# Node work of an attention pass cut into pieces behind the next round's groups, and matmuls of zeros left out

## What is computed

```python
h = (x @ W).reshape(N, H, D)                       # N = 12500, H = 4, D = 64
alpha = leaky_relu(a_src[src] + a_dst[dst], 0.2)   # per edge and head, self loops too
alpha = exp(alpha - amax[dst])
alpha = alpha / (segment_sum(alpha, dst)[dst] + 1e-16)
out = segment_sum(h[src] * alpha[:, :, None], dst)
x = layernorm(x + (out.reshape(N, H*D) + bias) @ Wl + bl)
```

## Time and profile before

| | us |
|---|---|
| median of 3 runs | 9799.77 (9795.94 to 9801.96) |
| the profiled execution | 9789.83, its span 9788.2 |
| attention pass, first to last aggregation (L844) | 204 to 2722 of the span |
| PE busy in the whole span | 6498.4 (66%) |
| POOL | 4718.8 (48%) |
| DVE | 4539.3 (46%) |
| ACT | 1864.8 (19%) |

### The profile page before, as it was taken

The page is one execution under the profiler, slowest core; times in us unless marked ns, Lnnn a source line. Parts: engine busy times, 40 slices in busy tenths (PEclk is TensorE's granted clock), DMA queues, the critical chain, the costliest instruction groups (busy, mean ns, idle before and its releaser), DMA issues.

```text
span 9788.2 us, 254659 instructions
## 1 busy us (share of the span) xinstructions
PE 6498.4 (66%) x65048; PEld 4741.4 (48%) x65049; DVE 4539.3 (46%) x11895; ACT 1864.8 (19%) x3800; POOL 4718.8 (48%) x4467
## 2 busy tenths in 40 slices
PE   4888777777726666665778866675776455455676
PEld 3666555555512221112444555664675454454566
DVE  4555555555578877774443333332222232232333
ACT  1433333333311334552000000000000000000000
POOL 2777666565500000004762036544764775774765
PEclk7888888888868889998889987887888677677788
DMA  2444444443310112334566566675776677677676
GB/s 56 100 97 95 94 91 94 92 89 87 87 33 39 79 80 116 131 138 171 174 185 191 177 221 203 221 230 172 226 253 209 208 276 266 207 259 243 211 268 231
DMA packets 973391, 1566.40 MB, mean 160 GB/s; under 512 B 499841, under 2 KB 621441, under 8 KB 966402
## 3 DMA queue, kind: packets, MB, share of 16 engines
q1 hardware_dynamic: 485762, 1244.14, 36.9%
q0 software_dynamic: 150016, 196.43, 9.7%
q10 hardware_dynamic: 337280, 122.87, 4.8%
HBM read 1337.91 MB, written 225.00 MB: 160 GB/s over the span
## 4 chain that ended last, share of the span: by engine, by line
PE 33%; issue 22%; DVE 15%; DVEq 11%; POOL 10%; DMA 7%; ACT 2%; ACTq 1%; SPq 0%; POOLq 0%
PE ps_turn L999 15%; POOL ARENA L671 10%; PE ps_turn L954 5%; PE ps_out L844 4%; DMA ARENA<-edge_attr 3%; DMA ARENA<-counts 2%; DVE ARENA L1886 2%; DVE ARENA L1884 2%; PE ps_pair L844 2%; PE ps_turn L817 1%; PE ps_pair L1021 1%; DVEq L1891 1%; DVEq L1981 1%; DVE ARENA L1981 1%; DVE DSUM L2050 1%
## 5 line engine op out<-in xcount | busy, mean ns | idle before, releaser
L999 PE MATMUL ps_turn<-ARENA 128*128 128x192 bf16 (+2 forms) x28812 | 2810.5, 267 | 834.6 <-DVE DSUM L2050 397.0
L999 PEld LDWEIGHTS ps_turn<-ARENA 128*128 128x128 bf16 x28812 | 2355.8, 108 | 1297.4 <-issue 996.4
L671 POOL DMA_INDIRECT ARENA<-table_sage,idx x1920 | 2013.1, 1048 | 1143.4 <-issue 963.6
L671 POOL DMA_INDIRECT ARENA<-table_gat,idx x1568 | 1693.8, 1080 | 851.9 <-issue 480.0
L954 PE MATMUL ps_turn<-ARENA 128*128 128x392 bf16 (+1 forms) x4204 | 1063.8, 359 | 679.7 <-DVE ARENA L1886 407.0
L671 POOL DMA_INDIRECT ARENA<-table_dev,idx x480 | 492.2, 1025 | 1616.6 <-ACT idx L1220 1472.3
L1884 DVE TENSOR_SCALAR ARENA<-ARENA 128x784 bf16<-128x784 f16 (+1 forms) x2102 | 1009.2, 480 | 363.5 <-issue 238.1
L954 PEld LDWEIGHTS ps_turn<-ARENA 128*128 128x128 bf16 (+1 forms) x4204 | 335.6, 101 | 1407.7 <-issue 1364.8
L671 POOL DMA_INDIRECT ARENA<-table_gine,idx x480 | 500.9, 1043 | 847.1 <-issue 684.0
L1202 ACT ACTIVATE ARENA<-ps_turn 128x784 f32 x784 | 645.9, 824 | 1086.4 <-PE ps_turn L954 1086.1
L2050 DVE TENSOR_REDUCE DSUM<-ps_turn 128x64 f32<-128x192 f32 (+2 forms) x686 | 263.9, 385 | 1171.7 <-PE ps_turn L999 966.3
(11 more groups left out here) (320 smaller groups left out, 5616.5 us busy)
## 6 DMA issues: line engine op xcount, KB each, us to landing
ARENA<-counts SPq DMA_DIRECT2D x1764, 448.0 KB
counts<-ARENA SPq DMA_DIRECT2D x49, 3136.0 KB, 9.0
ARENA<-counts SPq DMA_DIRECT2D x588, 224.0 KB
ARENA<-dst_b SPq DMA_DIRECT2D x393, 256.0 KB
ARENA<-edge_attr ACTq DMA_DIRECT2D x392, 128.0 KB
ARENA<-table_sage,idx POOLq DMA_INDIRECT x1920
ARENA<-table_gat,idx POOLq DMA_INDIRECT x1568
nodes_dev<-table_rows ACTq DMA_DIRECT2D x14, 672.0 KB
```

The lines of the kernel that those rows point to most:

```text
L671: pool.indirect_dma_start(ps["buf"][:, s, c, 0:ps["row"]], None, ps["table"][:, :], bass.IndirectOffsetOnAxis(idx[:, s, c:c + 1], 0)).then ...
L999: last = pe.matmul(ps_dense[half][:, 0:n], RING[:, b, :], XP[:, b, :], start=(b == PIECE_AT[pieces[0]]), stop=(j == pieces[-1] and b == PI ...
```

## The change

1. `fill` and its calls are gone: PE waits without matmuls of zeros in front of its waits.
2. The second half of a block's node work is owed (a register `owed` on PE, ACT and DVE is set to 1 behind `dense`) and paid in the next round, each piece at a fixed group `s` of the eight, on DVE and ACT behind that group's own instructions: the product on PE ahead of group 1's own work; on DVE the sum with x and bias and the mean at 2, the spread at 3, the norm and the side-by-side layout at 5, the split into parts at 6; the square root on ACT at 4, cut and stores at 7. Each piece stands in a test of `owed`, in every round. At a block's end the whole half stands once more, in a test, for a block that no round followed.
3. The product goes to `ps_turn` (the place of the transposes) instead of a corner of the bank of `expand`, and the sum `y` into `big` instead of `tmp`; `gat_normalise` waits for one more `rows_free`, that is until ACT has cut the block before.

```diff
+PRODUCT_AT, MEAN_AT, SPREAD_AT, ROOT_AT, NORM_AT, PARTS_AT, ROWS_AT = 1, 2, 3, 4, 5, 6, 7
-        ps_gat = ps_exp_all[:, 64:64 + TB * D]
+        ps_gat = ps_turn[:, 0:TB * D]
+        def owes(eng, owed):
+            return eng.If(eng.snap(owed, min_val=0, max_val=1) > 0)
         def sweep(...):                      # at the end of a block:
+                with owes(eng, owed):
+                    late(b - 1)
+                    settle(eng)
+                dense(b)
+                eng.reg_mov(owed, 1)
+            late(BLOCKS - 1)
         # TensorE
-            def fill(n):
-                for _ in range(n):
-                    pe.matmul(ps_fill, ZERO[:, :], ZERO[:, :], start=True, stop=True)
-                    fill(5)                  # expand, in front of logit_ready
-                        fill(5)              # expand, in front of each nodehot_ready
-                            fill(6)          # in front of messages_ready
+                        if s == PRODUCT_AT:
+                            with owes(pe, owed):
+                                gat_product(pe, before)
+                                pe.reg_mov(owed, 0)
         # ScalarE, behind the group's last instruction
+                    if s == ROOT_AT:
+                        with owes(act, owed):
+                            node_root(0, before)
+                    if s == ROWS_AT:
+                        with owes(act, owed):
+                            node_rows(0, before, before)
+                            act.reg_mov(owed, 0)
         # VectorE, behind the group's last instruction
+                        for piece, at in enumerate((MEAN_AT, SPREAD_AT, NORM_AT, PARTS_AT)):
+                            if s == at:
+                                with owes(ve, owed):
+                                    late_step.start(before, LATE_STEPS)
+                                    node_vector(ve, late_step, k, split, before, before, pieces=(piece,))
+                                    settle(ve)
+                                    if piece == 3:
+                                        ve.reg_mov(owed, 0)
         # gat_normalise
-            ve.wait_ge(rows_free, b + 1)
+            ve.wait_ge(rows_free, b + 2)
```

## The result

The changed kernel takes 9908.9 us (median) where the kernel before takes 9800.9 beside it: a ratio of 1.0112, interval 1.0094 to 1.0129, so 110 us slower by that ratio (108 between the medians). 9714 was predicted, with 9605 to 9850 as the range. The profiled execution of after has a span of 9906.6 us at a mean granted clock of 0.807 (before 9788.2 at 0.834). In the trace the attention pass, from the first sum (L844 before, L839 after) to the last, grows from 2518.5 to 2655.2 us, that is by 137. Behind the last sum 12 us of it come back: the last rows of the pass are cut 39.9 us after that sum before, and 27.5 us after it in the changed kernel.

The account below looks back on a forecast made before the run. Gathers bound rounds 0 to 12, then the loop of PE, DVE and ACT, with at most 366 us to gain. Terms -195 + 140 - 140 + 76 + 33 = -86 gave 9704 profiled, 9714 us median; range 9605 to 9850.

Parts of the forecast that it names:

- In rounds 0 to 12 nothing: Start of the attention pass: the gathers on POOL set the pace, so shorter work on other engines gains nothing there.
- Block ends, -195: Ends of blocks 1 to 13: the second half leaves them, gaining 15 us at each of 13, 195 us.
- The pieces, +140: Node work moved into the rounds on DVE, PE and ACT: costs 10.8 us per block, 140 us; bounds 65 to 220.
- Zeros, -140: PE's three batches of zero matmuls in front of waits: removing them gives their time back in full, 140 us.
- clock, +76: PE's sums in the rounds: without zeros 42% of the time at 1.2 GHz, not 20%, costing 76 us; bounds 0 to 275.
- The wait for the second `nodehot`: DVE's wait for PE within a group: removing two batches of five zeros shortens 79 waits by 0.56 each, 44 us.
- the wait for sums: DVE's wait for PE's sums: removing all three batches of zeros shortens 63 waits by 0.90 each, 57 us.
- Tests and tables, +33: In every round: DVE's four tests cost 28 us, ACT's extra table load in front of group 5's exponent 5 us.
- The moves: Product moved to `ps_turn` and `y` into `big`: costs nothing, as the instructions stay the same.
- A: Rival on PE: 80% of sums at 1.2 GHz, clock costs 207 us, 9845 us, slower than before; chance 0.12.
- B: Rival on DVE: one more instruction-fetch stop per round costs 103 us, 9817 us, no gain; chance 0.07.
- C: Rival in the rounds: pieces fall into waits and cost 5 us per block, not 10.8, giving 9639 us; chance 0.21.

Follow-up runs that it names:

- e5: The changed kernel with the three batches of zeros put back, issued as fewer, wider matmuls: ratio 1.0037 to the kernel before, +36 us.
- e2: The kernel before without its three batches of zeros, nothing else changed: 9895.9 us, ratio 1.0091, +89 us.
- e6: The kernel before plus tests of a never-set owed and the pieces' unused code, with zeros as fewer, wider matmuls: ratio 1.0020, +20 us.
- e7: The kernel before with its zeros issued as fewer, wider matmuls, nothing else changed: ratio 0.9999, -1 us.
- e8: The kernel before with twice as many zeros in each batch (10, 10 and 12), in wide matmuls: ratio 1.0051, +50 us.
- e1: The changed kernel with the three batches of zeros (5, 5 and 6 matmuls) put back, pieces kept: ratio 1.0069 to the kernel before, +68 us.
- e4: The kernel before, zeros included, plus tests of a never-set owed and the pieces' unused code in the rounds: ratio 1.0066, +65 us.
- e11: e5 with 16 more zeros on TensorE in groups 3, 4, 6 and 7 of a paying round: ratio 1.0014 to the kernel before, +14 us.
- e9: e5 with root, third and fourth piece, cut and stores one group earlier: ratio 1.0001 to the kernel before, +1 us.

## Why the prediction was wrong, point by point

The step that failed is the pair of terms for the zeros and the clock. Together they were to give 64 us; taking the zeros out cost 74 us (after less e5), and 89 in the kernel before alone (e2).

By runs the change divides into tests +20 (e6), block ends and pieces together +16 (e5 less e6) and zeros out +74 (after less e5); they add up to 110 by construction. The forecast had +33, -55 and -64.

**What bounds the kernel.** "In rounds 0 to 12 nothing" failed. They lost 46 us: some 13 with tests (e6 against e7) and 21 with the zeros out (e2); no run places the other 12. POOL was the pace there, but with a lead so small that a loop only some us per round slower makes it wait for slots.

**Block ends, -195.** Right in kind, too large: sum to sum 32.1 us in e6 and 19.3 in e5, 12.8 × 13 = -166. The first end of the trace before, the model for what would be left, had 15.9 us; in after the transposes alone take 2.41 to 3.22 us at the first two ends, where they took 1.72 and 1.70 before.

**The pieces, +140.** Mis-sized: 14.5 × 13 = 189. DVE's four cost 2.2, 1.8, 2.2 and 2.2 us, 8.4 of their 9.1; the -2.5 for waits that DVE would be spared hardly came. The product cost 3.4 (2.5 forecast), ACT's two parts 3.0 (1.7), of which the stretched load of the spans is the greater part. That load's 3.95 us at block ends stood in the trace of before; I did not look at the sequencers' rows. -166 and 189 make +23, and 16 was measured, with the wide interval above.

**Zeros, -140, and clock, +76.** These failed worst. The share: I turned a granted clock of 0.77 into 42% of sums. The clock was near that (0.74 to 0.79), but 186 of 280 sums were low, 66%, because part of the high level falls on the waits behind long sums, as the windows above show. And the zeros did not "come back in full": where they are gone PE waits instead. Waits of PE in e2, 844 to 2804:

```profile
PE ps_pair L877 <- DVE ARENA L1727: 140.6, 167, 1.6
PE ps_out L833 <- DMA ARENA<-edge_attr: 108.1, 74, 2.5
PE ps_pair L871 <- DVE ARENA L1748: 44.5, 27, 3.8
...
PE ps_pair L833 <- DMA ARENA<-edge_attr: 39.2, 24, 2.1
```

and in the kernel before, 826 to 2720:

```profile
PE ps_pair L879 <- DVE ARENA L1730: 64.2, 124, 1.0
PE ps_out L833 <- DMA ARENA<-edge_attr: 53.4, 70, 1.5
PE ps_pair L872 <- DVE ARENA L1751: 43.6, 22, 3.0
PE ps_pair L833 <- DMA ARENA<-edge_attr: 29.4, 32, 1.9
```

These four come to 332 us in e2 and 191 before: 142 us in which zeros had stood beside a wait that is there anyway (in after, where the pieces add to them, 406). DVE's waits for PE in e2 answer the term itself:

```profile
DVE ARENA L1727 <- PE ps_pair L877: 181.0, 85, 4.4
...
DVE ARENA L1681 <- PE ps_out L844: 122.7, 73, 3.4
DVE ARENA L1681 <- PE ps_pair L844: 32.5, 26, 2.5
```

The wait for the second `nodehot`, which was to give 44 us, stays at 181 where it was 184; the wait for sums, which was to give 57, grows from 81 us in 63 waits to 155 in 99 (126 in 80 in after). Only the wait in front of the logits fell, from 34 us to 10.

How e2's +89 divides between the low clock and the queue time of the zeros is not shown. With the forecast's 1.23 us for a low sum, its 110 more low sums would cost 135 us and, with 21 more in rounds 0 to 12, leave an estimated -67 for the zeros, half of the 140; e8, at the same price, gives +83 for another set of them. But the runs don't confirm that price: round 21 takes 47.5 us before with two low sums, and with six 50.4 in after and 47.7 in e2. Over the ten rounds that neither pay nor end a block, e2 has 3.2 more low sums per round than before and takes 1.8 us longer: 0.55 us each, net of what the missing zeros give back.

**Tests and tables, +33.** 20 (10 to 28): the right size, but in part by luck, as some 13 of it fell in rounds 0 to 12, for which the term had nothing. **The moves:** no row speaks against "nothing".

**Rivals.** A, the low clock, was the right mechanism, and its turning point of two thirds of the sums is what happened (66%). I gave it 0.12 because the level rises again after long sums; it does, and what comes behind them is a wait. Even so A's 9845 is under the measured time, since its other terms were the forecast's. B, a stop for instructions, did not come on DVE: the 20 us of e6 leave no room for its 103. Its kind came on PE, in e1 and e4 only. C, pieces hidden in waits, is refuted by the 14.5 us. The Trainium skill's advice in "TensorE: Matmul & The Clock Gate", section "Why this matters for your kernels", against idle gaps between bursts was the rule that spoke against this change, and e2 bears it out: +89 us.

What stays open: how the loss without zeros divides between clock and queue, how the 20 us of the tests divide between the tests and ACT's table loads, and where e11's gain and part of e9's lie.

## What to carry to other kernels

Before you take idle work out of TensorE, count what share of its long operations would run at the low level, cut at their own starts and ends; a mean clock over a stretch flatters it, because the fast part can fall on waits. Where a block's end is long, look first for an order at that end which lets the restart run beside the rest (one engine's two steps exchanged gave 38 us), and only then spread its work over the rounds, where it pays tests, longer code and disturbed waits. Read the sequencers' rows too: jumps and register loads there were worth 2 to 5 us each.

## What the hardware showed that I had not expected

- TensorE's jump at a block's end took 0.22 us or 4.86 with the same tests in the loop and only fewer or more instructions for the zeros (e6 and e4).
- VectorE's load of ten registers, 1.08 us in 86 of 98 cases before, takes 3.63 to 3.95 at the 12 ends where ScalarE has just stored rows, and 1.10 at most where the stores (and three other steps) are a group earlier (e9).
- In a round of the changed kernel TensorE ran six of eight sums at about 0.6 of its clock, and the stretches between them, mostly waits, at 0.95 to 1.00.
